# Where the value products of an attention key tile stand: in one run, or in three pieces behind three score products

## The chip, the cores and the metric

The kernel runs on one core of a Trainium2 chip. The metric is device time in microseconds (us) of one execution; lower is better. A time is given as the median of several runs of the same program.

## What is computed

The reference is a small early-fusion model: a token embedding part, a text embedding part, one attention layer with 32 heads of width 16, and a mixture of eight experts. Only the attention matters here. Cut to that:

```python
bsz, tgt, H = hidden_states.shape            # 4, 640, 512
Q = (proj(q_weight, WQ, q_bias) * scaling).reshape(bsz, tgt, HEADS, HEAD_DIM)
K = proj(k_weight, WK, k_bias).reshape(bsz, tgt, HEADS, HEAD_DIM)
V = proj(v_weight, WV, v_bias).reshape(bsz, tgt, HEADS, HEAD_DIM)
attn = jnp.einsum('bqhd,bkhd->bhqk', Q, K)
probs = jax.nn.softmax(attn, axis=-1)
ctx = jnp.einsum('bhqk,bkhd->bqhd', probs, V).reshape(bsz * tgt, H)
```

There are 4 x 32 = 128 heads in all, each with 640 queries, 640 keys, a width of 16 and a softmax over the keys.

## The kernel before

The program goes through four stages, one after the other: rows and projections, attention (`attend`), routing, experts. The change lies in `attend` alone, and there in the instructions of TensorE and in one position of ScalarE.

**Groups and key tiles.** The 128 heads are worked off as 32 groups of four heads (`GH = 4`, `NG = 32`). The 640 keys of a group are five key tiles of 128 (`KT = 5`). Of the 640 query columns 512 fill one PSUM bank; the last 128 (`REST`) of all four heads share another bank. So a key tile has five banks of scores (`U1 = 5`): one for each head with its first 512 columns, and one with the last 128 columns of all four. A group has 25 such units (`U2`).

**Two passes of score products.** The first pass (`first_pass`, L1378 and L1381) computes scores with the queries on the partitions, so that VectorE can take the maximum over the keys (L1468, L1470). The 20 columns of negative maxima of a group are made (L1473), transposed by TensorE (L1371), copied to SBUF by VectorE (L1455) and sent by a DMA on ScalarE's queue (`put_max`, L1517) into a row of the stacked queries `qs`. The second pass (`second_pass`, L1396 and L1399) computes the scores again with the keys on the partitions; the row of maxima is contracted along, so that ScalarE needs only an exponential (`exps`, L1505) from the PSUM bank into `pT`. Each pass has three PSUM banks in rotation: a first product waits until VectorE has reduced the bank three units back, a second product until ScalarE has taken the bank three units back.

**Value products.** `add_values` (L1403 to L1416) multiplies the exponentials of a key tile with the values `vs`, in float32, and accumulates over the five key tiles in two PSUM banks `pv`. Each head is one 32-column tile of the array, so the four heads of a piece stand side by side in the array. The query columns are done in two pieces, `PIECES = [(0, 512), (512, 128)]`: four matmuls of 512 columns, then four of 128, one run of eight for each key tile, 160 runs in all. Each matmul is recorded as two passes, so that a run has 16 records. The value matmuls have a column tile of 32 (the second field of `128*32` in the trace), the score products use all 128 columns (`128*128`, `96*128`).

**Order on TensorE.** It is written out by `group`: for each unit `s` of the second pass of group `c`, one unit (once two) of the first pass of the groups `c + 1` and `c + 2`, then the second product `s`, and in every fifth step a run of value products:

```python
second_pass(i, c, s, static)
kt, after = divmod(s - LAG - (U1 - 1), U1)
if after == 0:
    if kt >= 0:
        add_values(i, c, kt)
    elif not static:
        add_values(i, c - 1, KT - 1)
```

With `LAG = 3` the runs stand behind the second products 2 (the last key tile of the group before), 7, 12, 17 and 22. A run waits for the exponentials of its key tile, and the first of a group also for the copy of the context of the group before (`s_oev`). The last matmul of a run raises `s_pv`.

**Order on ScalarE.** `group` of ScalarE does the 25 exponentials; behind number `CTX_AT = 3` it copies the finished context of the group before out of `pv` (`copy_context`, L1511), which waits for `s_pv`; behind number `PUT_AT = 17` it issues the DMA of the next group's maxima. The exponential that opens a key tile waits until the value products of two key tiles back are done, because `pT` has two buffers.

**Others that look at `s_pv` and `s_oev`.** SyncE's queue stores the context of a group and then loads the inputs of the group three ahead (13 DMAs), after waits on `s_oev` and `s_pv`. GpSimd prepares one part of the expert weights for every five value runs (L1342 to L1350).

Of the kernel before, what the change touches and what calls it, by code (L numbers as in the profile page):

```python
# [31 lines left out]
T = COMPS * P  # L32
# [65 lines left out]
def early_fusion_kernel(nc, a, out):  # L98
    ctx = ExitStack()
    with ctx:  # L100
# [99 lines left out]
        def load_inverses(sp, b):  # L200
            for i in range(IT):
                at = (b * IT + i) * (HEADS // IT)
                sp.dma_start(den[:, b % 2, i], d_sum[at:at + HEADS // IT].unsqueeze(1).broadcast_to([HEADS // IT, HD, T])
                             ).then_inc(s_ctx[b], 16)

        attend(nc, a, locals())
        route(nc, a, locals())
        middle.close()
# [966 lines left out]
def attend(nc, a, g):  # L1175
# [12 lines left out]
    GH = 4  # L1188
    NG = B * HEADS // GH
    KT = T // P  # L1190
    REST = T - 512
    U1, U2 = GH + 1, (GH + 1) * KT
# [3 lines left out]

    PARTS = [(0, 0), (0, 1), (0, 2), (1, 0), (1, 1), (2, 0)]
    LOADS = 2 * len(PARTS) + 1
    PIECES = [(0, 512), (512, T - 512)]
    CTX_AT = 3  # L1200
    LAG = 3
    LEAD = 16
    PUT_AT = 17
    R = 4
    NI = NG // R
    SPLIT_PACE = 5
    ctx = ExitStack()
    with ctx:
        def sb(name, shape, dt=F32):
            return ctx.enter_context(nc.sbuf_tensor(name, shape, dt))  # L1210

        def sem(name):
            return ctx.enter_context(nc.semaphore(name))
# [3 lines left out]
        vs = [sb(f"vs{u}", [P, KT, GH * 32]) for u in range(R)]  # L1217
# [11 lines left out]
        pv = ps[:, 6:8].rearrange("p n t -> p (n t)")  # L1229
# [5 lines left out]
        s_s, s_p, s_pv = sem("scores"), sem("probs"), sem("values_added")  # L1235
        s_oev = sem("context_copied")
# [7 lines left out]
        def num(i, c):  # L1244
            return R * i + c
# [7 lines left out]
        def first_bank(c, s):  # L1253
            return mbank[(s + M1 * (c % R)) % len(mbank)]

        def second_bank(c, s):
            return sbank[(s + U2 * (c % R)) % len(sbank)]

        def behind(bank, units, c, s):

            at = (R + c % R) * units + s
            return next(d for d in range(1, at) if bank(*divmod(at - d, units)) == bank(c, s))
# [94 lines left out]
        @block.tensor  # L1357
        def _(pe):
            def first_pass(i, c, slot, static=False, turn=TURN):


                u, n, d = c % R, M1 * num(i, c) + slot, behind(first_bank, M1, c, slot)
                if not static or n >= d:
                    pe.wait_ge(s_mfree, n - d + 1)
                out = ps[:, first_bank(c, slot)]
                if slot == turn:
                    if static and c == 0:
                        pe.transpose(out[0:GH * KT, 0:P], ident[:, 0:GH * KT], ident[:]).then_inc(s_m, 1)
                        return
                    pe.wait_ge(s_nmr, num(i, c))  # L1370
                    pe.transpose(out[0:GH * KT, 0:P], nm[(c - 1) % 2][:], ident[:]).then_inc(s_m, 1)  # L1371
                    return
                if slot == 0:
                    pe.wait_ge(s_ld[u], 16 * LOADS * (i + c // R + 1))
                qt, h = divmod(slot - (slot > TURN), U1)
                q = slice(qt * P, (qt + 1) * P)
                if h < GH:
                    mm = pe.matmul(out, qs[u][0:STACK, h, q], ks[u][0:STACK, h, 0:512], start=True, stop=True)  # L1378
                else:
                    for h in range(GH):  # L1380
                        mm = pe.matmul(out[:, h * REST:(h + 1) * REST], qs[u][0:STACK, h, q], ks[u][0:STACK, h, 512:T],  # L1381
                                       start=True, stop=True)
                mm.then_inc(s_m, 1)

            def second_pass(i, c, s, static=False):

                u, n, d = c % R, U2 * num(i, c) + s, behind(second_bank, U2, c, s)
                if not static or n >= d:
                    pe.wait_ge(s_p, n - d + 1)
                if s == 0:  # L1390
                    pe.wait_ge(s_nm[c % 2], 16 * (R // 2 * i + c // 2 + 1))
                kt, h = divmod(s, U1)
                out = ps[:, second_bank(c, s)]
                k = slice(kt * P, (kt + 1) * P)
                if h < GH:
                    mm = pe.matmul(out, ks[u][:, h, k], qs[u][:, h, 0:512], start=True, stop=True)  # L1396
                else:
                    for h in range(GH):
                        mm = pe.matmul(out[:, h * REST:(h + 1) * REST], ks[u][:, h, k], qs[u][:, h, 512:T],  # L1399
                                       start=True, stop=True)  # L1400
                mm.then_inc(s_s, 1)

            def add_values(i, c, kt):  # L1403

                u = c % R
                pe.wait_ge(s_p, U2 * num(i, c) + U1 * (kt + 1))
                if kt == 0:
                    pe.wait_ge(s_oev, num(i, c))
                src = pT[(u + kt) % 2]
                for at, n in PIECES:  # L1410
                    for h in range(GH):
                        rows = slice(32 * h, 32 * h + 32)
                        col = 512 * h + at if at < 512 else 512 * GH + REST * h
                        mm = pe.matmul(pv[rows, at:at + n], vs[u][:, kt, rows], src[:, col:col + n],  # L1414
                                       start=kt == 0, stop=kt == KT - 1, tile_position=(0, 32 * h))
                mm.then_inc(s_pv, 1)  # L1416

            def group(i, c, static=False, following=2):

                ahead = [(c + 1, slot) for slot in range(LEAD, M1)] if following >= 1 else []  # L1420
                ahead += [(c + 2, slot) for slot in range(LEAD)] if following >= 2 else []
                for s in range(U2):
                    for cc, slot in ahead[s * M1 // U2:(s + 1) * M1 // U2]:
                        first_pass(i, cc, slot)
                    if following == 1 and s == M1 - LEAD + 3:
                        first_pass(i, c + 2, 0, turn=0)
                    second_pass(i, c, s, static)
                    kt, after = divmod(s - LAG - (U1 - 1), U1)
                    if after == 0:
                        if kt >= 0:  # L1430
                            add_values(i, c, kt)
                        elif not static:
                            add_values(i, c - 1, KT - 1)

            pe.wait_ge(s_setv, 4)
            pe.wait_ge(s_setg, 4)
            pe.sem_inc(s_pv, 1)
            for slot in range(M1):
                first_pass(0, 0, slot, static=True)
            for slot in range(LEAD):  # L1440
                first_pass(0, 1, slot, static=True)
            group(0, 0, static=True)
            with pe.Fori(0, NI - 1) as i:
                for c in range(1, R + 1):
                    group(i, c)
            for c in range(1, R):
                group(NI - 1, c, following=min(2, R - 1 - c))
            add_values(NI - 1, R - 1, KT - 1)

        @block.vector  # L1450
        def _(dve):
# [45 lines left out]
        def _(act):  # L1497
            def exps(i, c, s):
                u, n = c % 2, U2 * num(i, c) + s
                kt, h = divmod(s, U1)  # L1500
                if h == 0:
                    act.wait_ge(s_pv, KT * num(i, c) + kt)
                act.wait_ge(s_s, n + 1)
                dst = pT[(u + kt) % 2][:, 512 * h:512 * (h + 1)]
                act.activation(dst, ps[:, second_bank(c, s)], ACT.Exp).then_inc(s_p, 1)  # L1505

            def copy_context(i, c):
                u = c % 2
                act.wait_ge(s_pv, KT * (num(i, c) + 1) + 1)
                act.wait_ge(s_ost[u], 16 * (R // 2 * i + c // 2) + 1)  # L1510
                act.copy(osb[u][:], pv[:, 0:T]).then_inc(s_oev, 1)  # L1511
# [8 lines left out]
            def group(i, c, first=False, put=TURN):  # L1520
                for s in range(U2):
                    exps(i, c, s)
                    if s == CTX_AT and not first:
                        copy_context(i, c - 1)
# [798 lines left out]
```

## Time and profile before

| | us |
|---|---|
| median of 3 runs | 1636.45 (1632.8 to 1639.46) |
| the profiled execution | 1634.87 |
| its span, first to last instruction | 1633.0 |
| attention stage within the span | about 393 to 1022 |

In the rows, times are in us unless marked ns. PE is TensorE's matmuls, PEld its weight loads, DVE is VectorE, ACT is ScalarE, POOL is GpSimd, SP is SyncE; a q behind an engine is the issue of a DMA on its queue. L1414 is line 1414 of the kernel. Matmuls are pipelined: a record of 0.38 us can be followed by the next one after 0.22 us, so the distance between starts tells what a product costs. In brackets stands the idle time ahead of an instruction and what ended it.

### The profile page before, as it was taken

The page shows a single profiled execution, that of the slowest core. Times are in us where ns is not written, and L with a number is a line of the kernel's source. Part 1 is how long each engine was busy: PE and PEld are TensorE (multiplying, and loading weights), DVE is VectorE, ACT ScalarE, POOL GpSimd, SP SyncE. Part 2 cuts the span into 40 slices and gives each one's busy share as a digit, 9 for nine tenths or more (in the row PEclk, how much of TensorE's full clock was granted, in tenths as well). Part 3 has the DMA queues.
Part 4 walks back from the last instruction along what each step waited for, and adds up shares of the span by engine and source line. Part 5 has one row for each costly group of instructions (what it writes and reads, how often), then busy time and mean ns, then how long its engine had stood idle before and what let it go on. Part 6 is the DMA issues. An engine that isn't in the chain of part 4 may idle for free. (4 is left out here: it accounts for less than half of the span.)

```text
span 1633.0 us, 29916 instructions
## 1 busy us (share of the span) xinstructions
PE 1250.6 (77%) x10109; PEld 725.9 (44%) x10230; DVE 1195.4 (73%) x2040; ACT 840.8 (51%) x1752; POOL 368.3 (23%) x229
## 2 busy tenths in 40 slices
PE   0248257838899999999997988328549999999993
PEld 0236223313344444444443433005447777777772
DVE  7985999978888888888886878379655555555551
ACT  3675323523667777677775757753114444444441
POOL 4000200021334443333330021100022323323321
PEclk9958668966999999999998999657569999999997
DMA  5000305996666777777654662654359999999965
GB/s 163 0 1 1 114 0 186 304 233 154 185 185 183 197 192 193 207 200 203 183 142 77 128 163 83 114 110 150 133 181 360 313 309 310 308 305 310 307 190 148
DMA packets 115228, 294.92 MB, mean 181 GB/s; under 512 B 20006, under 2 KB 54822, under 8 KB 104676
## 3 DMA queue, kind: packets, MB, share of 16 engines
q1 hardware_dynamic: 90396, 210.09, 42.7%
q0 software_dynamic: 23712, 81.28, 18.6%
q10 hardware_dynamic: 1056, 2.79, 0.5%
q8 instruction: 30, 0.49, 0.1%
q14 instruction: 34, 0.28, 0.1%
HBM read 208.85 MB, written 90.32 MB: 183 GB/s over the span
## 5 line engine op out<-in xcount | busy, mean ns | idle before, releaser
L1505 ACT ACTIVATE pT<-p 128x512 f32<-128x512 f32 x800 | 422.3, 607 | 194.3 <-PE p L1396 107.8
L1468 DVE TENSOR_REDUCE mxa<-p 128x1 f32<-128x512 f32 x640 | 409.6, 681 | 106.0 <-PE p L1378 105.5
L1378 PE MATMUL p<-ks,qs 96*128 96x512 bf16 x640 | 255.1, 401 | 45.2 <-DMA vs<-d_v 24.1
L1396 PE MATMUL p<-qs,ks 128*128 128x512 bf16 x560 | 217.1, 388 | 33.0 <-DMA qs<-nmT 22.3
L1414 PE MATMUL p<-pT,vs 128*32 128x128 f32 (+1 forms) x2560 | 207.3, 442 | 1.4 <-ACT pT L1505 1.4
L2160 PE MATMUL p<-x,w 128*128 128x256 bf16 (+1 forms) x1728 | 145.5, 246 | 0.0
L2160 PEld LDWEIGHTS p<-x,w 128*128 128x128 bf16 x1728 | 133.5, 98 | 13.8
L1414 PEld LDWEIGHTS p<-pT,vs 128*32 128x32 f32 x2560 | 67.1, 109 | 154.2 <-issue 109.7
L2130 POOL DMA_INDIRECT d_acc<-yo,slot_row x47 | 74.6, 1588 | 266.7 <-DVE yo L2278 233.0
L1378 PEld LDWEIGHTS p<-ks,qs 96*128 96x128 bf16 x640 | 62.5, 98 | 148.7 <-DVE mxa L1468 59.3
L1346 POOL CAST xT<-xT 128x2048 bf16<-128x2048 f32 x24 | 45.4, 1891 | 300.4 <-PE p L1414 288.6
L2263 DVE SCALAR_TENSOR_TENSOR sg<-p,b,sg 128x256 f32<-128x256 f32 (+1 forms) x112 | 49.4, 441 | 83.3 <-ACT sg L2214 83.2
L1470 DVE TENSOR_REDUCE mxb<-p 128x4 f32<-128x512 f32 x160 | 108.8, 680 | 0.7 <-PE p L1381 0.7
L2160 PE MATMUL p<-x,shared 128*128 128x256 bf16 x960 | 108.2, 275 | 0.8 <-ACT x L2197 0.8
L2214 ACT ACTIVATE sg<-p,b1s 128x256 f32<-128x256 f32 (+1 forms) x112 | 49.1, 438 | 108.6 <-PE p L2160 108.6
L2160 PEld LDWEIGHTS p<-x,shared 128*128 128x128 bf16 x960 | 94.7, 99 | 14.8 <-ACT x L2197 1.1
L2219 ACT CAST y<-yf 128x256 bf16<-128x256 f32 (+1 forms) x112 | 41.5, 370 | 112.3 <-DVE yf L2265 112.3
L1396 PEld LDWEIGHTS p<-qs,ks 128*128 128x128 bf16 x640 | 63.0, 98 | 79.6 <-ACT pT L1505 38.7
L1348 POOL TENSOR_TENSOR xT<-xT 128x2048 bf16<-128x2048 f32 x24 | 97.8, 4073 | 2.1
L2267 DVE TENSOR_TENSOR y<-yf,y 128x256 bf16<-128x256 f32 (+1 forms) x112 | 42.9, 383 | 48.9 <-ACT y L2219 48.9
L431 PE MATMUL p<-ring 128*64 128x32 f32 x256 | 21.0, 254 | 74.3 <-DVE ring L541 74.3
L149 POOL DMA_INDIRECT wTq<-d_x,slot_token x47 | 47.9, 1019 | 121.1 <-DVE slot_token L2020 99.4
(413 smaller groups left out, 1981.3 us busy)
## 6 DMA issues: line engine op xcount, KB each, us to landing
w<-d_w SPq DMA_DIRECT2D x18, 2048.0 KB, 10.0
d_w<-xT POOLq DMA_DIRECT2D x24, 1024.0 KB, 6.4
shared<-d_w SPq DMA_DIRECT2D x10, 2048.0 KB, 7.7
w<-d_w SPq DMA_DIRECT2D x18, 1024.0 KB, 10.8
xT<-in_w1T POOLq DMA_DIRECT2D x16, 1024.0 KB, 10.8
qs<-d_q SPq DMA_DIRECT2D x192, 80.0 KB, 3.6
ks<-d_k SPq DMA_DIRECT2D x192, 80.0 KB, 3.7
d_v<-xT SPq DMA_DIRECT2D x20, 512.0 KB, 4.6
```

Of the source, the lines that this page charges most:

```text
L149: pool.indirect_dma_start(xg[n % RING][:, q], None, d_x2, bass.IndirectOffsetOnAxis(slot_token[:, j:j + 1], 0)).then_inc(s_xg[n % RING], 16)
L1348: pool.tensor_tensor(lo, wf[u], hi, ALU.subtract).then_inc(s_wsp, 1)
L1378: mm = pe.matmul(out, qs[u][0:STACK, h, q], ks[u][0:STACK, h, 0:512], start=True, stop=True)
L1396: mm = pe.matmul(out, ks[u][:, h, k], qs[u][:, h, 0:512], start=True, stop=True)
L1414: mm = pe.matmul(pv[rows, at:at + n], vs[u][:, kt, rows], src[:, col:col + n], start=kt == 0, stop=kt == KT - 1, tile_position=(0, 32 * h))
L1468: dve.tensor_reduce(mxa[u][:, h, qt:qt + 1], bank, AX.X, ALU.max, negate=True).then_inc(s_mfree, 1)
L1470: dve.tensor_reduce(mxb[u][:, :, qt], bank.rearrange("p (h k) -> p h k", h=GH), AX.X, ALU.max, negate=True).then_inc(s_mfree, 1)
L1505: act.activation(dst, ps[:, second_bank(c, s)], ACT.Exp).then_inc(s_p, 1)
L2130: pool.indirect_dma_start(d_acc, bass.IndirectOffsetOnAxis(slot_row[:, j:j + 1], 0), yo[j % OUTS][:], None, compute_op=ALU.add).then_inc(s ...
L2160: mm = pe.matmul(out, w[c][:, k, ws, t, cols], x[c][:, t, xs, 0:rows], start=t == 0 and m == 0, stop=t == IT - 1 and m == 2)
L2214: act.activation(sg[o % 2][:, 0:rows], ps[:, 2 + o, 0:rows], ACT.Sigmoid, scale=1.702, bias=b1s[c][:, 0, o:o + 1]).then_inc(s_sg, 1)
L2263: dve.scalar_tensor_tensor(gated, gate, b1[c][:, 0, o:o + 1], gated, ALU.add, ALU.mult).then_inc(s_u, 1)
```

## The change

The run of each key tile is split into three pieces by query columns: 0 to 256, 256 to 512 and 512 to 640. Each piece is four matmuls, one for each head. The three pieces of a key tile stand behind three successive second products (behind 2, 3 and 4; 7, 8 and 9; 12, 13 and 14; 17, 18 and 19; 22, 23 and 24) instead of all behind the first of the three. Only the first piece waits on semaphores, and only the last one raises `s_pv`. Columns 256 to 512 share the bank of columns 0 to 256, so only the first of these two sets the start flag. ScalarE's copy of the context moves from behind exponential 3 to behind exponential 4.

```diff
-    PIECES = [(0, 512), (512, T - 512)]
-    CTX_AT = 3
+    PIECES = [(0, 256), (256, 256), (512, T - 512)]
+    CTX_AT = 4
...
-            def add_values(i, c, kt):
+            def add_values(i, c, kt, piece):
 
                 u = c % R
-                pe.wait_ge(s_p, U2 * num(i, c) + U1 * (kt + 1))
-                if kt == 0:
-                    pe.wait_ge(s_oev, num(i, c))
+                if piece == 0:
+                    pe.wait_ge(s_p, U2 * num(i, c) + U1 * (kt + 1))
+                    if kt == 0:
+                        pe.wait_ge(s_oev, num(i, c))
                 src = pT[(u + kt) % 2]
-                for at, n in PIECES:
-                    for h in range(GH):
-                        rows = slice(32 * h, 32 * h + 32)
-                        col = 512 * h + at if at < 512 else 512 * GH + REST * h
-                        mm = pe.matmul(pv[rows, at:at + n], vs[u][:, kt, rows], src[:, col:col + n],
-                                       start=kt == 0, stop=kt == KT - 1, tile_position=(0, 32 * h))
-                mm.then_inc(s_pv, 1)
+                at, n = PIECES[piece]
+                for h in range(GH):
+                    rows = slice(32 * h, 32 * h + 32)
+                    col = 512 * h + at if at < 512 else 512 * GH + REST * h
+                    mm = pe.matmul(pv[rows, at:at + n], vs[u][:, kt, rows], src[:, col:col + n],
+                                   start=kt == 0 and at % 512 == 0, stop=kt == KT - 1 and (at + n) % 512 in (0, REST),
+                                   tile_position=(0, 32 * h))
+                if piece == len(PIECES) - 1:
+                    mm.then_inc(s_pv, 1)
...
-                    if after == 0:
+                    if after < len(PIECES):
                         if kt >= 0:
-                            add_values(i, c, kt)
-                        elif not static:
-                            add_values(i, c - 1, KT - 1)
+                            add_values(i, c, kt, after)
+                        elif kt == -1 and not static:
+                            add_values(i, c - 1, KT - 1, after)
...
-            add_values(NI - 1, R - 1, KT - 1)
+            for piece in range(len(PIECES)):
+                add_values(NI - 1, R - 1, KT - 1, piece)
```

## Rows read from the trace of the kernel before

**Rows 1.** Stretch 460 to 840 us: PE, PEld, DVE, ACT, POOL busy, clock, DMA.

```profile
460.00:840.00 380.00, 358.64 (x3141) 159.26 (x3190) 320.11 (x535) 270.26 (x516) 143.38 (x77) 1.00 0.69 193
```

**Rows 2.** Groups by line, 460 to 840 us; columns as in the page's part 5.

```profile
L1505 ACT ACTIVATE pT<-p 128x512 f32<-128x512 f32 x496 | 261.2, 607 | 109.7 <-PE p L1396 62.9 <-remote 45.5
L1468 DVE TENSOR_REDUCE mxa<-p 128x1 f32<-128x512 f32 x396 | 253.4, 680 | 59.2 <-PE p L1378 58.9
...
L1470 DVE TENSOR_REDUCE mxb<-p 128x4 f32<-128x512 f32 x100 | 67.9, 679 | 0.0
...
L1511 ACT COPY osb<-p 128x640 f32<-128x640 f32 x20 | 13.7, 686 | 0.0
L1473 DVE TENSOR_TENSOR nm<-mxa,mxb 128x20 f32<-128x20 f32 x19 | 11.1, 586 | 0.7
...
L1455 DVE CAST nmT<-p 20x128 bf16<-20x128 f32 x20 | 5.4, 269 | 0.0
```

**Rows 3.** Timeline of PE over two key tiles: start, length, line, operands, count.

```profile
707.00 0.38 PE L1396 MATMUL p<-qs,ks 128*128 128x512 bf16 x1
707.32 1.28 PE L1414 MATMUL p<-pT,vs 128*32 128x512 f32 x16
708.53 0.39 PE L1378 MATMUL p<-ks,qs 96*128 96x512 bf16 x1
708.76 0.38 PE L1396 MATMUL p<-qs,ks 128*128 128x512 bf16 x1
...
710.46 0.38 PE L1396 MATMUL p<-qs,ks 128*128 128x512 bf16 x1
710.77 1.28 PE L1414 MATMUL p<-pT,vs 128*32 128x512 f32 x16
...
714.30 1.28 PE L1414 MATMUL p<-pT,vs 128*32 128x512 f32 x16
```

**Rows 4.** Weight loads inside the value run of 707.32, each at the start of a pass.

```profile
707.77 0.13 PEld L1414 LDWEIGHTS p<-pT,vs 128*32 128x32 f32 x4 [0.30 <-issue]
708.20 0.13 PEld L1414 LDWEIGHTS p<-pT,vs 128*32 128x32 f32 x4 [0.30 <-issue]
```

**Rows 5.** PE's transposition of the maxima, first and last of nineteen in a row.

```profile
478.07 0.27 PE L1371 MATMUL p<-ident,nm 128*20 128x128 f32 x1
...
823.96 0.27 PE L1371 MATMUL p<-ident,nm 128*20 128x128 f32 x1
```

**Rows 6.** Who PE waited for, 393 to 1022 us: total, times, longest.

```profile
PE p L1396 <- DMA qs<-nmT: 22.3, 24, 2.9
PE p L1378 <- DVE mxa L1468: 14.9, 9, 11.1
PE p L1396 <- ACT pT L1505: 10.1, 40, 0.7
```

**Rows 7.** Timeline of one group: its first product, products 7 and 17, the next group's first.

```profile
717.99 0.39 PE L1396 MATMUL p<-qs,ks 128*128 128x512 bf16 x1 [0.91 <-DMA qs<-nmT]
...
722.78 0.39 PE L1396 MATMUL p<-qs,ks 128*128 128x512 bf16 x1 [0.22 <-ACT pT L1505]
...
729.76 0.38 PE L1396 MATMUL p<-qs,ks 128*128 128x512 bf16 x1
...
735.99 0.39 PE L1378 MATMUL p<-ks,qs 96*128 96x512 bf16 x1
736.82 0.39 PE L1396 MATMUL p<-qs,ks 128*128 128x512 bf16 x1 [0.44 <-DMA qs<-nmT]
```

**Rows 8.** Timeline of ACT in that group: around the context's copy, and the maxima's DMA.

```profile
721.53 0.69 ACT L1511 COPY osb<-p 128x640 f32<-128x640 f32 x1
...
730.27 0.73 ACTq L1517 DMA_DIRECT2D qs<-nmT  x1
```

**Rows 9.** Waits of SP's queue and of POOL in the stage: total, times, longest.

```profile
SPq L1280 <- ACT osb L1511: 356.6, 29, 38.2
...
POOL xT L1346 <- PE p L1414: 288.6, 23, 31.9
```

## The prediction, made before the changed kernel ran

> **What bounds the kernel now.** I read the stage's busy times first, then the groups by line, the timeline of TensorE, and last the waits. In the steady part of the attention stage TensorE is busy 358.64 of 380 us at a granted clock of 1.00, while VectorE is busy 320.11 and ScalarE 270.26 of these 380 [rows 1]. By the groups, a group of four heads costs VectorE 25 x 0.680 + 0.586 + 0.269 = 17.9 us and ScalarE 25 x 0.607 + 0.686 = 15.9 us [rows 2]. The nineteen transpositions of the maxima from 478.07 to 823.96 enclose 18 groups, so a group takes 345.89 / 18 = 19.22 us [rows 5]. TensorE's own work is read between starts: from the run at 710.77 to the one at 714.30 a key tile passes with no wait in 3.53 us [rows 3], so five take 17.65. TensorE therefore sets the pace, and the missing 19.22 - 17.65 = 1.57 us per group (50 us over 32 groups) are its waits.
>
> Of these waits the rows name three kinds [rows 6]. The DMA of the maxima holds a group's first product 24 times, 22.3 us in all; full PSUM banks on ScalarE's side stop it 40 times, 10.1 us; VectorE 9 times, 14.9 us, of which 11.1 are one wait. A recorded product outlasts its slot by 0.16 us (0.38 recorded, 0.22 to the next start [rows 3]), so each wait costs some 0.16 us more than its figure; over 73 waits that is 12 us. Leaving the single 11.1 out, the sum is 36.2 + 11.5 = 48 us, near the 50 found from the pace.
>
> **The price of a run.** A score product takes 0.22 us from start to start. With a run of value products in between, the distance is 708.53 - 707.00 = 1.53 [rows 3], so a run takes 1.31 us of TensorE's time. Its four heads stream side by side: the second pass starts at 707.77 and the third at 708.20, thus 0.43 us for 512 columns [rows 4]. A run has two such passes and two of 128 columns (0.107 each), together 1.07 us of streaming. The other 0.24 is paid once per run: 0.10 on entry (0.32 from the last score product to the run instead of 0.22), 0.02 more in the first pass (0.45 against 0.43), and 0.12 on exit (708.20 to 708.53 is 0.33, of which 0.21 streams) [rows 3, 4]. These 0.24 belong to going from products of full width to 32-column tiles and back: between two pieces of 512 and 128 columns inside the run nothing of the kind stands, since the third pass follows the second after its 0.43.
>
> The page TensorEngine Tiling of the Trainium skill (section Key Properties) says that a change of tiling mode drains the engine; the gaps of 0.10 and 0.12 agree with it. The page TensorE: Matmul & The Clock Gate (section Measured speedup vs the span model) speaks the other way: a pack costs the duration of one matmul and about 4 ns per further tile, which by estimate would make two more pieces cost some 0.02 us, 4 us over the stage in place of the 77 below. Between the two pages the rows decide for the drain.
>
> **The change, part by part.**
> - *Two more switches per key tile.* Three pieces stream the same 1.07 us and pay 0.24 three times: 1.79 instead of 1.31, or 0.48 more. Over 160 key tiles this is 77 us; a group of TensorE's own work becomes 17.65 + 5 x 0.48 = 20.05 us. Nothing hides it, since TensorE is the pacing engine. No row shows a run of 256 columns; the low bound is that entry costs a later piece nothing, since it has no wait on a semaphore (0.14 x 2 = 0.28 per key tile), the high bound the full 0.48. I take 0.48, as the entry is the same at both runs shown, 0.32 and 0.31 (710.46 to 710.77) [rows 3].
> - *Waits for ScalarE's banks.* Now up to five pairs of products 0.44 us apart follow each other against exponentials of 0.607, and after the context's copy (0.69 at 721.53 [rows 8]) product 7 comes 0.22 late at 722.78 [rows 7]. With pieces behind three of every five second products at most three of these products follow each other at 0.44, and three banks hold them. I take these waits as gone: 10.1 + 40 x 0.16 = 16 us.
> - *The wait for the maxima.* In the group of rows 7 product 17 comes 11.77 us after the first, the DMA is issued 0.51 later (730.27 [rows 8]), and the next first product starts 6.55 after the issue: 7.06 from product 17, set by the DMA. TensorE would have been ready at 735.99 + 0.22 = 736.21, or 6.45 after product 17. Two key tiles' values stand in that last part, so its own work grows by 0.96 to 7.41, past the DMA; the wait of 0.61 goes. Three stand in the first part, which grows by 1.44 less the ScalarE wait of 0.38: 12.83. The group's sum is 12.83 + 7.41 = 20.24, near the floor of 20.05.
> - *VectorE.* At 17.9 per group it has 2 us of slack, so most of its short waits (3.8 us) go. The one of 11.1 stays: a single hold-up late in the stage, not TensorE's pace.
> - *The copy moved behind exponential 4.* The last key tile's third piece starts 0.31 after product 4 and the copy can follow exponential 4, some 1.1 us after product 4's start; it ends at 1.8. The next group's first piece stands behind product 7, three pairs and one piece later: 0.45 + 3 x 0.44 + 0.31 = 2.1. The copy is covered by 0.3 us; if that cover goes, TensorE waits up to 0.69 per group.
> - *Semaphores.* `s_pv` rises two units later. ScalarE's first exponential of a key tile needs a piece that now ends one pair ahead of its score product, so it does not wait. SP's queue idles 356.6 us for the context and POOL 288.6 for `s_pv` [rows 9]; a shift of some 1.5 us per group lies inside that. PUT_AT and the DMA counts stay. Weight loads rise by half, of 0.13 us each, beside streaming passes of 0.21; free.
>
> **The sum.** Floor 20.05, group of rows 7 20.24. I take 20.24 as the pace, 1.02 more than 19.22, over 32 groups 33 us: 77 of cost, 44 of the waits given back. The profiled execution's 1634.87 becomes 1668; the median of the runs stands 1.6 higher, which is inside the noise.
>
> **Rivals.**
> - *The waits stay.* The DMA's landing may move with the group, as a wait often does, and the banks may fill as before. Against it: the last part's own work passes 7.06. If none of the 50 us comes back: 1634.87 + 77 = 1712.
> - *A new wait on the copy.* If ScalarE lags behind at exponential 4, the first piece waits for all of the 0.69 us copy: 22 us more, 1690. For it speaks that the cover is only 0.3.
> - *No change.* The entry's 0.10 is in truth the wait for the exponentials, which only the first piece has. Then 0.28 per key tile, 17.65 + 1.4 = 19.05, and with the same 0.19 over the floor 19.24: about 1635. Against it: that gap is the same at both runs of rows 3, whereas waits vary.
> - *Faster.* A piece that returns to score products at once pays no switch, because the products next to it overlap with it. Then the floor stays 17.65, the bank waits of 0.38 go, and the group of the maxima's DMA sets the pace: 11.77 - 0.38 + 7.06 = 18.45 in rows 7, whose group took 18.83; 0.38 to 0.6 per group, so 12 to 19 us, at best 1616. It decides where the two added switches cost less than about 0.06 us each; rows 3 show 0.24. The span model of the page TensorE: Matmul & The Clock Gate (Part 3) would lead to this rival.
>
> **Chances.** Forecast 0.76, waits stay 0.08, wait on the copy 0.09, no change 0.04, faster 0.03. By itself the forecast runs from 1655 (no wait left, 1661, and the 320 added switches 0.02 us cheaper each) to 1685 (0.5 us per group of waits left). The range is drawn from 1652 to 1692, so that the wait on the copy is inside; left out are the full 1712, no change and faster. Half a per cent, about 8 us, is what a measurement can tell from no change: faster 0.03, same 0.04, slower 0.93.
>
> **What would show it.** Right: 480 runs of 8 value records each; 0.31 us into each piece and the same 0.12 after it; 0.88 between the score products around a 256-column piece and 0.67 around the 128; TensorE's waits for the maxima and for ScalarE mostly gone; transpositions 20.0 to 20.5 us apart. Wrong: a distance near 0.65 around a 256-column piece (no switch price), first pieces waiting for the copy, or waits for the maxima as long as before.

## The result, and the profile after

The change makes the kernel slower: 1710.64 us (1706.67 to 1714.43, 4 runs) against 1637.95, a ratio of 1.0448 (95% interval 1.0413 to 1.0484), or 73 us. The sign was as forecast; the size was not. The forecast was 1668, the range ended at 1692.

The switches cost what the prediction said. The timeline of TensorE over one key tile of the changed kernel, with its three pieces (they are now L1415):

```profile
700.90 0.38 PE L1378 MATMUL p<-ks,qs 96*128 96x512 bf16 x1
701.12 0.38 PE L1396 MATMUL p<-qs,ks 128*128 128x512 bf16 x1
701.43 0.64 PE L1415 MATMUL p<-pT,vs 128*32 128x256 f32 x8
702.00 0.39 PE L1378 MATMUL p<-ks,qs 96*128 96x512 bf16 x1
702.23 0.38 PE L1396 MATMUL p<-qs,ks 128*128 128x512 bf16 x1
702.54 0.64 PE L1415 MATMUL p<-pT,vs 128*32 128x256 f32 x8
703.11 0.40 PE L1381 MATMUL p<-ks,qs 96*128 96x128 bf16 x4
703.35 0.39 PE L1399 MATMUL p<-qs,ks 128*128 128x128 bf16 x4
703.66 0.43 PE L1415 MATMUL p<-pT,vs 128*32 128x128 f32 x8
704.02 0.39 PE L1378 MATMUL p<-ks,qs 96*128 96x512 bf16 x1
```

Each piece starts 0.31 us after the score product ahead of it (701.12 to 701.43), and the distance around a piece of 256 columns is 702.00 - 701.12 = 0.88, around the one of 128 columns 704.02 - 703.35 = 0.67. These are the predicted 0.88 and 0.67; each piece pays the 0.24 of [rows 3, 4].

The waits changed as predicted too, and others came. TensorE's waits in the whole stage after the change, in total, times and longest, answering to [rows 6]:

```profile
PE p L1378 <- DVE mxa L1472: 31.6, 24, 11.8
PE p L1378 <- issue: 16.8, 11, 2.9
PE p L1396 <- DMA qs<-nmT: 4.6, 5, 2.6
...
PE p L1415 <- ACT pT L1509: 0.3, 1, 0.3
PE p L1415 <- ACT osb L1515: 0.3, 1, 0.3
```

The maxima's DMA fell from 22.3 us in 24 waits to 4.6 in 5. ScalarE's 10.1 us fell to 0.3, and the copy of the context cost 0.3 once. But first products now wait 31.6 us for VectorE instead of 14.9, and there is a wait of 16.8 us that nothing in the profile ends ("issue"), which the kernel before did not have on L1378. The transpositions of the maxima show the pace [rows 5], here in four groups in a row:

```profile
618.62 0.28 PE L1371 MATMUL p<-ident,nm 128*20 128x128 f32 x1
...
639.66 0.28 PE L1371 MATMUL p<-ident,nm 128*20 128x128 f32 x1
...
660.96 0.28 PE L1371 MATMUL p<-ident,nm 128*20 128x128 f32 x1
...
686.03 0.28 PE L1371 MATMUL p<-ident,nm 128*20 128x128 f32 x1
```

An ordinary group takes 21.04 to 21.30 us, not 20.24, and the one that opens a turn of TensorE's loop 25.07 (up to 26.96 at other turns). So there are two new costs: about 1 us in each group, and 4 us or more in each turn of the loop, which holds four groups.

**The microsecond in each group.** The timeline around VectorE's combination of the maxima, in the changed kernel:

```profile
702.16 4.08 POOL L1348 TENSOR_TENSOR xT<-xT 128x2048 bf16<-128x2048 f32 x1
...
704.27 2.00 DVE L1477 TENSOR_TENSOR nm<-mxa,mxb 128x20 f32<-128x20 f32 x1
...
706.93 0.39 PE L1378 MATMUL p<-ks,qs 96*128 96x512 bf16 x1 [0.86 <-DVE mxa L1472]
```

This operation on 20 columns took 0.586 us before [rows 2] and takes 2.00 now. It ends at 706.27, just as GpSimd's subtraction ends (702.16 + 4.08 = 706.24). The same pair in the kernel before:

```profile
703.23 4.08 POOL L1348 TENSOR_TENSOR xT<-xT 128x2048 bf16<-128x2048 f32 x1
...
706.76 0.59 DVE L1473 TENSOR_TENSOR nm<-mxa,mxb 128x20 f32<-128x20 f32 x1
```

There too it ended with the subtraction: 707.35 and 707.31. So most of the 0.59 was never VectorE's own work (experiment 1: 0.18). The overlap merely was short, and the change made it longer: `s_pv`, which starts GpSimd's part, rises two units later in the group.

**The four microseconds in each turn.** The timeline of TensorE at the start of a loop turn, changed kernel:

```profile
850.93 0.61 PE L1378 MATMUL p<-ks,qs 96*128 96x512 bf16 x1 [2.92 <-issue]
851.76 0.63 PE L1378 MATMUL p<-ks,qs 96*128 96x512 bf16 x1 [0.22 <-issue]
852.18 0.63 PE L1396 MATMUL p<-qs,ks 128*128 128x512 bf16 x1
```

and the row of the stretch behind it, whose last columns are the granted clock, the DMA share and GB/s:

```profile
851.50:853.50 2.00, 1.78 (x5) 0.46 (x3) 1.60 (x3) 1.19 (x2) 0.00 (x0) 0.50 0.00 0
```

TensorE stands 2.92 us without a reason in the trace, and then works at a granted clock of 0.50, its lower level of 1.2 GHz: products are 0.43 us apart instead of 0.22. The queue that loads instructions tells why. First its row (packets, MB, share) before, then after:

```profile
q8 instruction: 30, 0.49, 0.1%
```

```profile
q8 instruction: 86, 1.41, 0.3%
```

In all 56 packets and 0.92 MB were added. Between 475 and 970 us the kernel before moved no packet on this queue; the changed kernel moves nine from one turn's gap to the next, here from 669.5 to 758.5:

```profile
q8 instruction: 9, 0.15, 0.7%
```

The seven turns have six jumps back, and a gap of 2.4 to 2.9 us stands at each of the six. Four groups now have 240 value matmuls instead of 160. The hypothesis: the longer loop body no longer stays loaded, is loaded anew in each turn, and the jump back waits for its first part.

### The profile page after: what moved, and what is told of

It reads as the page before. It is cut to its first block and busy times, and to the rows that moved or that the text cites. A ratio compares the mean times of both kernels' runs of the same rounds, so it can differ in the third digit from the quotient of the medians.

```text
span 1704.8 us, 32447 instructions
## 1 busy us (share of the span) xinstructions
PE 1312.2 (77%) x11360; PEld 724.1 (42%) x11510; DVE 1245.7 (73%) x2040; ACT 862.6 (51%) x1752; POOL 367.6 (22%) x229
## 3 DMA queue, kind: packets, MB, share of 16 engines
q8 instruction: 86, 1.41, 0.3%
## 5 line engine op out<-in xcount | busy, mean ns | idle before, releaser
L1509 ACT ACTIVATE pT<-p 128x512 f32<-128x512 f32 x800 | 444.2, 600 | 248.8 <-PE p L1396 119.7
L1472 DVE TENSOR_REDUCE mxa<-p 128x1 f32<-128x512 f32 x640 | 415.7, 685 | 81.3 <-PE p L1378 71.7
L1378 PE MATMUL p<-ks,qs 96*128 96x512 bf16 x640 | 258.6, 407 | 81.8 <-DVE mxa L1472 32.8
L1415 PE MATMUL p<-pT,vs 128*32 128x256 f32 (+1 forms) x3840 | 277.6, 362 | 8.3 <-ACT pT L1509 0.3
L1396 PE MATMUL p<-qs,ks 128*128 128x512 bf16 x531 | 206.1, 392 | 5.2 <-DMA qs<-nmT 4.6
L1378 PEld LDWEIGHTS p<-ks,qs 96*128 96x128 bf16 x640 | 63.1, 99 | 224.6 <-DVE mxa L1472 112.7
L1415 PEld LDWEIGHTS p<-pT,vs 128*32 128x32 f32 x3840 | 76.4, 108 | 154.9 <-issue 83.4
L431 PE MATMUL p<-ring 128*64 128x32 f32 x256 | 21.7, 258 | 73.8 <-DVE ring L541 73.8
```

Source lines behind the costliest of these rows:

```text
L1472: dve.tensor_reduce(mxa[u][:, h, qt:qt + 1], bank, AX.X, ALU.max, negate=True).then_inc(s_mfree, 1)
```

## The experiments

Theory: 73 us are three costs, of which only the first was predicted: the switches (about 30), the clash of VectorE with GpSimd (about 25) and the reload of the loop (about 26); the three estimates add up to 81, somewhat too much. The rivals ascribe the new waits to the order of the pieces itself.

**1. GpSimd two key tiles later, in the changed kernel.**

```diff
-                pool.wait_ge(s_pv, SPLIT_PACE * n + 1)
+                pool.wait_ge(s_pv, SPLIT_PACE * n + 3)
```

> The changed kernel, with GpSimd's preparation of a part of the expert weights starting two key tiles later (it waits for 5n + 3 value runs instead of 5n + 1). Theory: in the changed kernel VectorE's small combination of the maxima takes 2.0 us instead of 0.58 because it cannot run beside GpSimd's subtraction, and TensorE loses 0.86 + 0.16 us per group by it. With the subtraction elsewhere it should take 0.18 us, groups that do not open a loop turn should fall from 21.04 to about 20.05 us, and over 24 groups the time should fall by about 25 us, to 1685. Rival: VectorE is late because of where the pieces stand, GpSimd has nothing to do with it; then the time stays at 1710 and the groups at 21.04.

Measured: 1699.22, ratio 1.0383 (1.0343 to 1.0424). The combination of the maxima (duration in ns as minimum, median, maximum) is as forecast:

```profile
L1477 DVE TENSOR_TENSOR nm<-mxa,mxb x32: 178/180/1329, 373.1 to 1061.1; 128x20 f32<-128x20 f32 x32
```

Ordinary groups fell to 20.11 us, against a forecast floor of 20.05. But only 11 us came back instead of 25, because the gap at each turn grew:

```profile
839.57 0.78 POOL L1334 DMA_DIRECT2D xT<-in_w1T  x1
...
845.93 0.61 PE L1378 MATMUL p<-ks,qs 96*128 96x512 bf16 x1 [5.15 <-issue]
...
932.07 0.39 PE L1378 MATMUL p<-ks,qs 96*128 96x512 bf16 x1 [2.76 <-issue]
```

It is now 5.1 to 5.4 us in five turns instead of 2.4 to 2.9. GpSimd issues a load of 1 MB just ahead of each of these five. The sixth gap has no transfer of GpSimd near it (its last was issued at 907.16), and stayed at 2.76. So it fits that these transfers delay the instructions, but it was not tried by itself. The theory of the clash holds.

**2. The same instructions in the old order.** The kernel before with three pieces back to back in one run: the longer body, but one switch per key tile.

```diff
-    PIECES = [(0, 512), (512, T - 512)]
+    PIECES = [(0, 256), (256, 256), (512, T - 512)]
...
-                                       start=kt == 0, stop=kt == KT - 1, tile_position=(0, 32 * h))
+                                       start=kt == 0 and at % 512 == 0, stop=kt == KT - 1 and (at + n) % 512 in (0, REST),
+                                       tile_position=(0, 32 * h))
```

> The kernel before, with the three pieces of 256, 256 and 128 columns back to back in one run at the old place: as many instructions as in the changed kernel, but only one switch per key tile. Theory: the longer loop body is loaded anew in each turn; the instruction queue should show about 86 packets instead of 30, every fourth group should open with a gap of 2.5 to 3 us that no engine ends, some 4 us per turn with the slower clock behind it, less what hides in the group's wait for the maxima; 20 to 28 us in all, so 1655 to 1665. The switches cost nothing here, so the other groups stay at 19.2. Rival: the gap at every fourth group comes from the order of the pieces; then this kernel stays at 1638.

Measured: 1687.9, ratio 1.0318 (1.0272 to 1.0364); 86 instruction packets; a distance around the run of 1.53 us, as with two pieces. The gap stands at each turn (2.9 to 5.1 us) though the order is the old one, so the rival falls. The cost is 3.18%, or 52 us, instead of 20 to 28. TensorE's waits show where a part of the rest is:

```profile
PE p L1396 <- DMA qs<-nmT: 32.8, 18, 4.1
PE p L1378 <- issue: 23.5, 6, 5.1
PE p L1378 <- DVE mxa L1469: 15.2, 9, 11.2
PE p L1396 <- ACT pT L1506: 8.2, 34, 0.7
```

Besides the gaps (23.5 us), the waits for the maxima grew from 22.3 to 32.8; what is left of the 52 was not priced. In one group, behind a gap, the DMA was issued at 677.56 and the product came at 686.63:

```profile
677.56 0.73 ACTq L1518 DMA_DIRECT2D qs<-nmT  x1
...
679.65 0.38 SPq L1275 DMA_DIRECT2D vs<-d_v  x1
...
686.63 0.61 PE L1396 MATMUL p<-qs,ks 128*128 128x512 bf16 x1 [2.95 <-DMA qs<-nmT]
```

That is 9.07 us from issue to product, against 6.55 in [rows 7, 8]. What made it late is open. No instruction packet started between the issue at 677.56 and 685.8. What does differ is the place of the last of SyncE's thirteen input loads: it is issued 2.09 us behind the maxima's DMA here, and 0.72 ahead of it in the group of rows 8 (730.27):

```profile
729.55 0.85 SPq L1275 DMA_DIRECT2D vs<-d_v  x1
```

**3. Two pieces behind two products.** The changed kernel with the old sizes: one added switch, no added instruction.

```diff
-    PIECES = [(0, 256), (256, 256), (512, T - 512)]
-    CTX_AT = 4
+    PIECES = [(0, 512), (512, T - 512)]
+    CTX_AT = 3
```

> The changed kernel with the old two pieces, 512 columns behind one score product and 128 behind the next: two switches per key tile, as many instructions as before. Theory: no gap at every fourth group and 30 packets on the instruction queue; one added switch of 0.24 us per key tile, 1.2 us per group, of which the wait for the maxima hides most: by the working of the prediction 11.77 + 0.72 - 0.38 + 7.06 = 19.2 us, plus 0.2 to 0.5 where the combination of the maxima runs into GpSimd's subtraction (about 1.3 us long instead of 0.58). 1637 to 1655. If the switches alone made the change slow, without help of the other two, it would be half of the 72 us slower: 1674.

Measured: 1643.63, ratio 1.0046 (1.0022 to 1.0071), 30 instruction packets. Nineteen transpositions give the pace:

```profile
478.32 0.28 PE L1371 MATMUL p<-ident,nm 128*20 128x128 f32 x1
...
831.88 0.28 PE L1371 MATMUL p<-ident,nm 128*20 128x128 f32 x1
```

(831.88 - 478.32) / 18 = 19.64 us per group, against 19.22 before: of 1.2 us of switches the wait for the maxima hid most, as its working said. The combination of the maxima took 1.33 us, as forecast. With no reload and a shorter clash, the added switch costs 0.46%, or 8 us; half of what the change with its two added switches cost would be 36.

**4. The loop written out.** TensorE's seven turns as straight code, in the changed kernel, and then together with the later GpSimd of experiment 1.

```diff
-            with pe.Fori(0, NI - 1) as i:
+            for i in range(NI - 1):
```

> The changed kernel with TensorE's loop over seven turns written out as straight code; the order of its work and every wait are the same. Theory: the gap that opens every fourth group stands at the jump back to the loop's start, because the longer body no longer stays loaded; straight code is loaded ahead of its use, so the gaps of 2.4 to 2.9 us and the slow clock behind them go, while the instruction queue still shows some 86 packets: about 26 us less than the changed kernel, 1684, and groups of 21.0 to 21.3 us throughout. Rival: loading more code is slow wherever it happens; then the time stays near 1710 or rises.

> The changed kernel with TensorE's loop as straight code and GpSimd's preparation two key tiles later, both suspected new waits taken away, the pieces as they are. Theory: what is left is the price of the two added switches alone, with the wait for the maxima covered: groups of 20.1 to 20.4 us, about 0.95 more than before over 32 groups, 30 us: 1665, the value of the prediction. Rival: there is a third cost; then it stays above 1680.

Measured: 1687.77, ratio 1.0307 (1.0244 to 1.0369), with groups of 21.04 to 21.7 us and no gap at a turn, apart from one of 22.6 where the maxima came late; and with both edits 1665.62, ratio 1.0170 (1.0108 to 1.0232). The packets were 69, where some 86 had been expected. With both suspected waits taken away the pace is

```profile
479.58 0.28 PE L1371 MATMUL p<-ident,nm 128*20 128x128 f32 x1
...
842.34 0.28 PE L1371 MATMUL p<-ident,nm 128*20 128x128 f32 x1
```

(842.34 - 479.58) / 18 = 20.15 us, and TensorE's longest waits in the stage are

```profile
PE p L1378 <- DVE mxa L1472: 14.4, 2, 11.7
PE p L1396 <- DMA qs<-nmT: 3.2, 2, 3.0
PE p L1378 <- DVE mxb L1474: 1.0, 3, 0.5
```

of which 11.7 is the single hold-up that the kernel before had as 11.1. Little is left but the switches: this is the kernel that the prediction described, and it takes the time that the prediction gave. The steps between the ratios are the three costs: 1.70% for the switches, less the waits that they gave back (28 us), 1.37% for the clash (22), 1.41% for the reload (23). By the intervals each of them is uncertain by 10 to 15 us. They also depend on the order of the edits: with the loop in place, taking the clash away gave only 11 us (experiment 1), because the gaps grew.

**5. The one run as straight code**, alone and with the DMA of the maxima behind exponential 15 instead of 17.

> Three pieces back to back in one run per key tile, with TensorE's loop as straight code. Theory: all of the 51 us that this order cost with the loop came from loading the loop's body anew, the waits for the maxima behind each gap included; as straight code it should be as fast as the kernel before, 1632 to 1642. Rival: four more matmuls per run cost something themselves; then some 5 us or more are left.

> Three pieces back to back in one run, TensorE's loop as straight code, and the DMA of the maxima behind exponential 15. Theory: the 30 us that the straight code kept over the kernel before come from the maxima's DMA, which lands up to 3 us later in groups in which code is loaded, and the old order has no slack there; with the DMA issued 1 us earlier half or more of it goes: 1630 to 1645, against 1622 for the same two changes' sibling with the short loop. Rival: the straight code itself starves TensorE, whatever the maxima do: 1650 or more.

Measured: 1665.96, ratio 1.0197 (1.0133 to 1.0260), and with the earlier DMA 1633.7, ratio 0.9970 (0.9936 to 1.0004). The first theory fell: straight code is not free in this order. The gap at the turns went, but TensorE's waits for the DMA of the maxima did not:

```profile
PE p L1396 <- DMA qs<-nmT: 26.3, 15, 3.6
...
PE p L1378 <- DMA qs<-nmT: 9.2, 5, 2.6
```

These are 35.5 us, against 22.3 in the kernel before, and not all of the 31 us. With the DMA issued earlier 10.5 and 2.8 us of them are left, and 2.3% of the time went. A load of code beside the DMA is not needed to make it late, though: from one issue at 665.46 to its product at 675.16, 9.70 us, no instruction packet moved. Why the DMA lands late in this order stays open. Against the same edit with the short loop (ratio 0.9921, below) about 0.5%, or 8 us, is left, hardly more than the intervals can tell; whether the straight code starves TensorE by that much stays open.

**6. The wait for the maxima in the kernel before**, alone and with the later GpSimd.

```diff
-    PUT_AT = 17
+    PUT_AT = 15
```

> The kernel before with the DMA of the maxima issued behind exponential 15 instead of 17. Theory: its landing sets the start of a group in the kernel before; issued 1.0 us earlier, the wait of 0.87 us at the head of a group goes, and a group takes 18.3 to 18.6 us instead of 19.2: 15 to 25 us less, 1613 to 1623. Rival: what ends the wait is the load of the other DMA traffic at that moment, and the DMA lands no earlier: 1638.

> The kernel before with the DMA of the maxima behind exponential 15 and GpSimd's preparation two key tiles later. Theory: the combination of the maxima falls from 0.58 to 0.18 us, VectorE needs 17.5 us per group, and what is left above TensorE's 17.65 is its waits for ScalarE and the maxima's DMA: 18.2 to 18.8 us per group, 1612 to 1623. Rival: GpSimd's transfers then run beside the maxima's DMA and delay it: 1625 to 1640.

Measured: 1622.5, ratio 0.9921 (0.9889 to 0.9953), and with both 1617.72, ratio 0.9897 (0.9872 to 0.9921). The prediction's reading of what held the old kernel was right: with the DMA one microsecond earlier a group takes 18.8 us, and the 24 waits of 22.3 us have become

```profile
PE p L1396 <- DMA qs<-nmT: 7.5, 5, 2.5
```

The last of the two is the fastest kernel of all, 1.0% below the kernel before.

**7. An added switch without cover:** two pieces, with both edits of experiment 6.

> Two pieces behind two successive score products, with the earlier DMA of the maxima and the later preparation by GpSimd. Theory: nothing hides an added switch here, so a group takes TensorE's own 17.65 + 5 x 0.24 = 18.85 us plus about 0.1, against 18.69 with one run; 18.95 x 32 gives about 9 us more than the sibling with one run, 1627. Rival: the split gives back the waits for ScalarE (12 us in the sibling) and more, so that it is as fast or faster: 1618 or less.

Measured: 1632.55, ratio 0.9967 (0.9942 to 0.9992), 0.70% or 11 us more than with one run (0.9897), where 9 had been forecast. TensorE's waits for ScalarE fell to 2.7 us in 8, but new ones for VectorE came (7.8 us in 14). Here too the split gives back less than its switches cost.

## Why the prediction was right and wrong

*Right.* The price of a switch held to the hundredth (0.31, 0.88, 0.67), and so did its consequence: TensorE's floor of 20.05 us per group, measured 20.11 where nothing else interferes. The waits for ScalarE and for the maxima went as worked out, the copy stayed covered, and both rivals on the other side fell. Experiment 4 gives 1665.62 for the forecast's own mechanism, against the forecast 1668; that they lie 2 us apart is closer than the interval (18 to 38 us above the kernel before) can vouch for. The rival in which the waits stay came near the measured time with 1712, but by luck: those waits went, and two others took their place.

*Wrong, first: the semaphores.* The step reads that `s_pv` rising two units later "lies inside" POOL's idle time. That POOL could wait was true and beside the point. Its start moved against the work of another engine. VectorE's combination of the maxima started 3.53 us into the subtraction before (706.76 - 703.23) and 2.11 after (704.27 - 702.16), so it waited 1.4 us longer, and TensorE stood 0.86 us behind it. VectorE's slack of 2 us per group did not help, since this is a single stall ahead of a PSUM bank that is due at once; so its short waits, which the step on VectorE took as gone, grew instead (31.6 us in 24, of which 11.8 are the single hold-up). The row had been there to read: 20 columns in 586 ns [rows 2] are too slow for the operation, which takes 178 when GpSimd is still. This term was priced at nothing and measured about 22 us.

The page SBUF — State Buffer of the Trainium skill (section Who interferes with whom) states it as a rule: a VectorE instruction with two SBUF inputs contends with a GpSimd instruction that reads SBUF, and the one issued second blocks until the first ends. The traces agree: the ends differ by 0.03 to 0.04 us in both kernels, and it is 0.18 us when GpSimd's work stands elsewhere.

*Wrong, second: the instructions.* The step called half as many weight loads again "free", since they lie beside streaming passes. For the array they do. For the loop body they and their matmuls are half as many value instructions again, and the body no longer stayed loaded: 9 packets loaded anew in each turn, a gap of 2.4 to 2.9 us, then the lower clock. This was not priced at all and measured about 23 us. The instruction queue of before (no packet between 475 and 970 us) would have shown that the body stayed loaded, and raised the question whether a longer one would.

On this the page Runtime: NRT & Kernel Launch of the Trainium skill (section Instruction fetch mechanics) says that a taken branch to code outside the loaded window forces a load ahead of execution, and that straight code streams with its loads mostly hidden. The first half agrees with experiments 2 and 4: gaps of 2.4 to 5.1 us at the jumps back, and none in straight code. The second agrees with experiment 4 (1.0170 without the clash); experiment 5 shows a straight code that cost 31 us in the order that waits on the maxima's DMA, and what of this the code's loads did is open.

## What to carry to other kernels

Price a split not only by what the pieces do on their own engine: count the instructions that it adds to a loop body, and look at the instruction queue's packets before and after. When a semaphore moves, ask what each engine that starts on it will then run beside, not only whether that engine has time. An operation that is slow for its size in the profile of before can be a hidden wait, and a later change can lengthen it.

## What the runs showed of the hardware

- A two-input VectorE operation of 178 ns took 0.59 us or 2.00 us, each time until GpSimd's 4.08 us subtraction ended (within 0.04 us).
- A longer loop body on TensorE was loaded anew in every turn, 9 packets of 16 KB each time (0.92 MB / 56); the shorter one moved none. The gap at the jump was 2.4 to 2.9 us, and 5.1 to 5.4 where GpSimd's loads had been moved close to it. Behind a gap the granted clock was 0.50.
- In the order with one run, the DMA of the maxima took 9.07 us from issue to product in a group behind such a gap, against 6.55. Why is open: the group's last input load was issued behind it instead of ahead of it, and no instruction packet started in its first 8 us.
